# More products of a constant in TensorE's waits, in a four-layer recurrent block of attention and gated layers

## Time and profile before

| | us |
|---|---|
| median of 3 runs | 4672.91 (4669.56 to 4678.95) |
| the profiled execution | 4681.39 |
| its span | 4679.6 |
| mean granted clock of TensorE in the span | 0.924 |
| TensorE busy | 3769.4 (81%) |
| VectorE busy | 2666.6 (57%) |
| ScalarE busy | 1891.5 (40%) |
| GpSimd busy | 782.5 (17%) |

### The profile page before, as it was taken

The page is one execution under the profiler, slowest core; times in us unless marked ns, Lnnn a source line. Parts: engine busy times, 40 slices in busy tenths (PEclk is TensorE's granted clock), DMA queues, the critical chain, the costliest instruction groups (busy, mean ns, idle before and its releaser), DMA issues. The chain is left out here.

```text
span 4679.6 us, 57461 instructions
## 1 busy us (share of the span) xinstructions
PE 3769.4 (81%) x20191; PEld 1899.0 (41%) x20355; DVE 2666.6 (57%) x5719; ACT 1891.5 (40%) x3814; POOL 782.5 (17%) x715
## 2 busy tenths in 40 slices
PE   5878888788887888887887888877888787887776
PEld 2344433435334443344433444343533444334434
DVE  5565556555566545664556555655556654566455
ACT  2443444343433434343344433444343343434324
POOL 0031101220012300222003120032101230012213
PEclk9989998999989999899998999899998999989987
DMA  4000010000000001000100001000000000100030
GB/s 139 28 8 22 5 34 28 15 14 11 28 28 28 1 18 36 20 22 1 39 28 8 22 5 34 28 9 21 11 28 28 28 1 16 36 23 22 1 81 19
DMA packets 79876, 113.86 MB, mean 24 GB/s; under 512 B 11452, under 2 KB 60167, under 8 KB 79047
## 3 DMA queue, kind: packets, MB, share of 16 engines
q1 hardware_dynamic: 73662, 101.08, 7.0%
q10 hardware_dynamic: 5898, 8.77, 0.6%
HBM read 80.68 MB, written 28.34 MB: 23 GB/s over the span
## 5 line engine op out<-in xcount | busy, mean ns | idle before, releaser
L704 DVE TENSOR_REDUCE nmax<-banks 128x1 f32<-128x512 f32 (+3 forms) x1216 | 761.1, 658 | 376.1 <-PE banks L543 208.9
L634 ACT ACTIVATE probs<-banks 128x512 f32<-128x512 f32 (+3 forms) x1536 | 673.7, 491 | 493.1 <-PE banks L561 489.9
L93 PE MATMUL banks<-filler,identb 128*128 128x512 bf16 x2384 | 689.3, 413 | 106.3 <-PEq L73 60.5
L543 PE MATMUL banks<-ks,qs 72*128 72x512 bf16 (+3 forms) x1536 | 472.0, 348 | 100.2 <-DVE nmax L704 70.2
L561 PE MATMUL banks<-qs,ks 74*128 74x512 bf16 (+3 forms) x1536 | 488.8, 352 | 39.9 <-ACT probs L634 21.5
L93 PEld LDWEIGHTS banks<-filler,identb 128*128 128x128 bf16 x2536 | 267.9, 107 | 412.2 <-issue 219.5
L599 PE MATMUL banks<-probs,v 128*32 128x512 f32 (+3 forms) x3072 | 352.9, 533 | 54.9 <-DVE att L691 33.4
L671 POOL TENSOR_SCALAR_AFFINE_SELECT probs<-probs 128x512 f32<-128x512 f32 x256 | 206.8, 809 | 1124.1 <-ACT probs L634 1124.1
L543 PEld LDWEIGHTS banks<-ks,qs 72*128 72x128 bf16 x1536 | 142.0, 101 | 427.9 <-DVE nmax L704 280.0
L333 POOL TENSOR_TENSOR rstd<-var,neghalf 128x4 f32<-128x4 f32 x24 | 24.3, 1011 | 1522.0 <-DVE var L261 1522.0
L561 PEld LDWEIGHTS banks<-qs,ks 74*128 74x128 bf16 x1536 | 144.4, 103 | 291.9 <-ACT probs L634 120.5
(11 more groups left out here) (410 smaller groups left out, 6065.8 us busy)
## 6 DMA issues: line engine op xcount, KB each, us to landing
qs<-parts_scratch SPq DMA_DIRECT2D x288, 96.0 KB
ks<-parts_scratch SPq DMA_DIRECT2D x288, 96.0 KB
parts_scratch<-parts SPq DMA_DIRECT2D x48, 384.0 KB, 2.8
qs<-max_parts SPq DMA_DIRECT2D x192, 4.0 KB
x<-in_x SPq DMA_DIRECT2D x9, 256.0 KB, 2.8
w_up_s<-in_w_up ACTq DMA_DIRECT2D x1, 2048.0 KB
x_scratch<-x SPq DMA_DIRECT2D x8, 256.0 KB, 3.7
factor_scratch<-att SPq DMA_DIRECT2D x8, 256.0 KB
```

Of the source, the lines that this page charges most:

```text
L93: nc.tensor.matmul(K.ps[:, bank, :], K.identb[:, :], K.filler[:, :], start=True, stop=True)
L543: mm = nc.tensor.matmul(K.ps[:, b, i * keys:(i + 1) * keys], K.qs[0:72, 4 * g + j, t * P:(t + 1) * P], K.ks[0:72, 4 * g + j, 0:keys], star ...
L634: nc.scalar.activation(probs[:, 4 * (q % QUADS) + m % 4, q0:T], K.ps[:, bank("second", m), q0:T], ACT.Exp, scale=scale).then_inc(exped, 1)
L704: nc.vector.tensor_reduce(nmax[:, t, h:h + len(heads)], K.ps[:, n % 2, 0:len(heads) * keys].rearrange("p (j k) -> p j k", k=keys), AX.X, A ...
```

## The change

The change adds constant products and nothing else; no transfer and no instruction of another engine is altered. In `down` of the experts a wait for an earlier value of the same semaphore is put in front of them. In the attention the wait for the bank that the next second score overwrites is moved in front of three products into that bank. The diff, cut to its lines:

```diff
@@ gated_layer_norm, TensorE
-            keep_busy(nc, K, 3, 18)
+            keep_busy(nc, K, 3, 26)
             for t in range(NT):
                 pe.wait_ge(xn_ready, t + 1)
...
-            keep_busy(nc, K, 3, 3)
+            keep_busy(nc, K, 3, 5)
@@ prepare, TensorE, layer 2
-                    keep_busy(nc, K, 3, 9)
+                    keep_busy(nc, K, 3, 12)
...
+                    keep_busy(nc, K, 3, 3)
                     pe.wait_ge(xrT_ready, 1)
@@ attention, TensorE (waits_first=10 in layer 1, 0 elsewhere)
+                keep_busy(nc, K, 5, waits_first)
                 beside.run(beside.on_tensor, -1)
...
                         mm.then_inc(oturned, 1)
+                        if causal and second:
+                            bank_read("second", second[0])
+                            keep_busy(nc, K, bank("second", second[0]), 3)
...
                             first_scores(n)
                             if causal and s < LAG:
-                                keep_busy(nc, K, 3, 1)
+                                keep_busy(nc, K, 3, 2 if n == first[0] and s else 1)
...
                     for q in weigh:
                         g, k = divmod(q, NT)
+                        if causal and s > 8 * NG + 1:
+                            keep_busy(nc, K, 0, 10 if q == 4 * NG - 1 else 2)
                         if causal:
                             pe.wait_ge(masked, q + 1)
...
                 if wo is not None:
+                    keep_busy(nc, K, 3, 4)
                     pe.wait_ge(att_ready, NG)
...
                     mm.then_inc(att_turned, 1)
+                    keep_busy(nc, K, 3, 3)
                     pe.wait_ge(attT_ready, 1)
@@ local_qkv, TensorE
     def tensor(pe, banks_free=None):
+        if L:
+            keep_busy(nc, K, 3, 4)
...
+        else:
+            keep_busy(nc, K, 3, 3)
         pe.wait_ge(shifted, 2)
...
             if t:
                 pe.wait_ge(v_copied, 3)
-                keep_busy(nc, K, 2, 8)
+                keep_busy(nc, K, 2, 14 if t == NT - 1 else 8)
+            else:
+                keep_busy(nc, K, 6, 8)
             turn(t)
@@ local_attention, TensorE
+                keep_busy(nc, K, 6, 4)
                 scores(0)
                 scores(1)
+                keep_busy(nc, K, 6, 3)
                 for w in range(UNITS):
                     if w + 2 < UNITS:
                         scores(w + 2)
+                    if w == 0:
+                        keep_busy(nc, K, 6, 5)
                     turn(w)
@@ Glu.tensor
+        keep_busy(nc, K, 3, 5)
         for t in range(NT):
             mm = nc.tensor.transpose(...)
...
+        keep_busy(nc, K, 3, 3)
         pe.wait_ge(self.shifted, 2)
...
+                    if self.alone:
+                        keep_busy(nc, K, 3, 3)
                     pe.wait_ge(self.hnT_ready, 1)
...
+                if self.alone:
+                    keep_busy(nc, K, 1, 5)
                 pe.wait_ge(self.hid_ready, 3)
...
         mm.then_inc(self.down, 1)
+        if self.alone:
+            keep_busy(nc, K, 1, 7)
@@ experts, TensorE
                 def down(e):
+                    if e == E3 - 1:
+                        pe.wait_ge(hid_ready, 2 * e + 1)
+                        keep_busy(nc, K, 0, 5)
                     pe.wait_ge(hid_ready, 2 * e + 2)
...
                 down(E3 - 1)
-                keep_busy(nc, K, 0, 14)
+                keep_busy(nc, K, 0, 22)
```

More of the change, by code:

```diff
@@ L472, in run_alone, with attention @@
     K.clear()
-def attention(nc, K, causal, wo=None, bo=None, combine=True, beside=None, after_store=False):
+def attention(nc, K, causal, wo=None, bo=None, combine=True, beside=None, after_store=False,
+              waits_first=0):
     (scored, reduced, turned, hi_ready, lo_ready, masked, rows, scored2, exped, weighed, oT_ready, oturned, vec,
@@ L1268, in __init__ @@
         self.nc, self.K, self.L = nc, K, L
+        self.alone = alone
         (self.back, self.vec, self.var_ready, self.rstd_ready, self.hn_ready, self.turned, self.hnT_ready, self.up,
@@ L1838, in batch_loop @@
                 prepare(nc, K, 1, beside=ffn)
-                attention(nc, K, True, K.w1_o, beside=ffn)
+                attention(nc, K, True, K.w1_o, beside=ffn, waits_first=10)
         with ExitStack() as two:
```

## The result

| | before | after |
|---|---|---|
| median | 4675.93 us (4 runs, 4669.56 to 4682.99) | 4754.03 us (4 runs, 4750.02 to 4763.5) |
| profiled execution | 4681.39 | 4750.02 |
| granted clock, mean of the span | 0.924 | 0.967 |
| TensorE busy | 3769.4 | 3991.6 |

The changed kernel takes 1.017 times as long (95% interval 1.0147 to 1.0192), some 78 us more. The forecast was 4713 us, some 40 more, with 4755 as the upper end of its range. The direction was right, and the loss is twice the forecast one.

What follows compares the result with a forecast made beforehand. A batch was taken as a chain through TensorE with short waits for others. Costs 17.3 less gains 12.3 gave +5.0 us a batch, 40 in eight: 4672.9 + 40 = 4713 us, own range 4690 to 4735, all cases 4658 to 4755.

Steps and rivals of the forecast that it cites:

- (1): Layer 2's causal attention: no cold stretch in its body, so added products only cost, 6.0 us a batch.
- (f): A batch's start: 6.8 us at low clock slow only 13 products, so a gain of 0.5 us a batch.
- (d): Normalized projections of layer 2 and the experts' start: cold stretches removed, gains of 1.0 and 1.6 us a batch.
- (4): Products that are a block's first work, operands ready after the barrier: 17 x 0.22 = 3.7 us cost a batch.
- (a): Start of layer 1, cold for 10.24 us: first scores must await their rows, so a gain of 1.4 us.
- (2): Layer 1's causal attention: products under busy VectorE are free, the rest cost 4.6 us a batch, 3.6 at the end.
- (b): Layer 1's second cold 10.24 us: 18.88 us against 16.21 for layer 2's same steps, a gain of 2.7 us.
- (c): Layer 1 behind the 2.71 us wait for VectorE: TensorE's chain cold 3.4 or 6.8 us, a gain of 1.9 us.
- Rival A: Faster, chance 0.22: cold stretches are dearer than forecast, net -2.8 us a batch, 4650 us.
- (3): Last turn of each local projection: six more products on the path cost 1.3 us, twice 2.6 a batch.
- Rival C: Clearly slower, chance 0.20: clock still falls at layer 1's two cold stretches, some products outlast waits: 4754 us.
- B: No change, chance 0.13: other engines' waits absorb the attention's products, costs fall by 5 us a batch: 4673 us.

Runs made afterwards that it cites:

- twelve alone: Kernel before with 12 products ahead of the first scores of each local attention: 4732.53 us, ratio 1.012.
- waits-only kernel: Changed kernel without the 102 products a batch shown on the path or beside layer 2's attention, the other 121 kept: 4628.56 us, ratio 0.9905.
- Eleven products: Kernel before with two products, not one, at the first score of each of layer 1's steps 1 to 11: 4655.25 us, ratio 0.9953.
- two mirror runs: Products at the experts' end: changed kernel with 14 instead of 22, 4756.45 us; kernel before with 22 instead of 14, 4681.31 us.
- the 40 alone: Kernel before with only the 40 added products in the body of layer 2's causal attention: 4747.5 us, ratio 1.0149.
- six and eleven products at the right two places: Kernel before with two products before each of layer 1's blocks 10, 11, 12: ratio 0.9939; with eleven in layer 1's steps 1 to 11: 0.9953.

## Why the prediction was half right

**What failed: the size of the sum.** Forecast +5.0 us a batch, measured +8.6. The steps that were mis-sized are (1), 6.0 and measured 7.2; (f), -0.5 and measured +0.6; the experts' part of (d), -1.6 and measured -0.75; and by less (4), 3.7 for 4.2, (a) and (e). Layer 1's attention gave 0.8 us back against them. Two errors stand behind these. The sum let every cold stretch that the products aim at go in all eight trips and let none come in a new place; the changed kernel has one at the start of layer 2's attention in two trips, in the experts' first part in four, at layer 1's start in three, and in its steps 12 to 24 in two. And (f) took idle time behind a barrier for a wait.

**Right: what bounds the kernel and that waits are the measure.** A product on the path costs 0.215 us (twelve alone), one in a wait nothing (twelve more in a wait of 3.12 us), and neither the number of products nor the clock decides alone: the waits-only kernel has 121 of them more than the kernel before, about the changed kernel's clock, and is 1% faster.

**Step (1), mis-sized: 6.0, measured 7.2, which is 6.35 and 0.85 that it did not have.** The ten before the last weighing were right (the last weighing starts 1.85 us later, forecast 1.9), and so were the 1.4 for the first steps with one turn's 0.6: in a trip without a cold stretch, up to the fourth group's first scores, the section grew from 37.1 to 39.1 us. What was a little too small is "the others": from that point to the last turn it is 4.3 us more against 0.6 + 1.9 + 1.5 = 4.0. The remaining 0.85 is a mean over trips: in two of eight the changed kernel has a cold stretch at the start of this attention, and takes 75.7 and 75.3 us. The forecast counted the cold stretches that go and none that come.

**Step (2) with (b) and (c), right but for the size of (c).** The end's costs are 3.9 for 3.6. (c) is 2.6 for 1.9. The steps 12 to 24, where the forecast had (b) less group 0's 0.6, are 2.1 us shorter in the mean, as forecast, but as a mix of 2.9 in six trips and nothing in two. Eleven products brought (b) alone, 3.4 us in seven of eight trips, a little over the 2.7 taken from the same steps of layer 2. Over the first steps the attention lost 0.9 and not 0.4. Rival A, faster by dearer cold stretches, failed on this: a cold stretch of TensorE costs what the same work at full clock saves, less what another engine's wait covers, not half its length.

**Steps (3) and (5), right, (4) nearly.** 2.7 for 2.6 and 0.4 for 0.4. In (4) the local blocks' fours cost 0.8 to 0.86 each, as counted; the lone gated block's five came to 1.6 instead of 1.1, as they ran cold in some trips.

**Step (a), 1.1 for 1.4.** The bound was the right one, a DMA ends the wait. But the rows land 9.6 us after the first issue, 749.61 to 759.23, and not the 9.0 taken from layer 2.

**Step (d), half failed.** The projections gave 1.05 of 1.0. The experts' first part is still cold in four of eight trips, where the forecast let it be warm in all: 0.75 of 1.6.

**Step (f), failed in its mechanism.** It put eight products into 5.53 us <-issue as into a wait. That is time behind a barrier: it starts when the last engine arrives. TensorE was the last already, by 0.3 us, so nothing was free. Forecast -0.5, measured +0.6 in its section; that this counts in the whole the two mirror runs did not show.

**The offset.** The forecast took 8.5 us off for the profiled execution of before standing above its median of three runs (5.5 above that of all four). The changed kernel's profiled execution stood 4 below its own. So of the 41 us between 4713 and 4754, 3.6 x 8 = 29 are the steps above, and 12 are where two single executions lie among their runs.

**Rival C had the number, and its mechanism only in a small part.** It gave 4754 because the clock would still fall in (a) and (b), which were to lose 4.1 us of gains. The clock does still fall there, but in few trips: (a) is cold for about 5 us in three of eight, (b) for 6.8 in two. (a) brought 1.1 for 1.4, and (b)'s steps gave in the mean what was forecast. That its figure is the measured one is luck. The loss is mostly products on the path at full clock, the forecast's own mechanism, with gains that were smaller than forecast. B, that other engines' waits absorb layer 2's products, is excluded by its section, 65.7 to 72.1 us with the 40 alone.

**The signs named ahead.** The batch's clock, 0.98 for 0.97; the last weighing, 1.85 for 1.9; layer 2's section, 6.3 for 6; layer 1's stretch, 15.8 for 16; the local projection's last turn, 1.29 for 1.3: as said. Two were off: the first scores of layer 1 come 7.4 us after the turn of x in the trip shown and 7.0 in the mean, not 6.8, and TensorE's busy time rose by 26 us in the batch shown, not over 30, as products at full clock took the place of cold work.

## What to carry to other kernels

Keep TensorE's clock up with constant products only where the trace shows an idle time that another engine or a DMA ends, one product per 0.216 us of it and no more; in front of each place ask what TensorE does next if the products are not there. Here 102 of 223, all but five of them without such a wait, cost more than all 223 gained, and turned a kernel that is 1% faster into one that is 1.7% slower; six and eleven products at the right two places brought 0.6% and 0.5% alone. Idle time behind a barrier is not a wait: products ahead of it are free only as long as another engine arrives later than TensorE, and here TensorE was the last already.

## What the runs showed that I had not expected

- Cold stretches move. Eleven products that made layer 1's middle warm left its end with the longer cold stretch in five trips and not three, and products in layer 2 alone changed layer 1's mean by 0.5 us. A section without a cold stretch repeats to a hundredth of a microsecond (65.72 and 65.70; 72.06 and 72.06), yet its mean over the trips does not (65.9 and 66.5; 73.1 and 72.3), and the sum of a kernel's sections drifts by one or two us a batch.
- The runs of one kernel lie wider than the first three showed: 4664 to 4689 us for the kernel before on one chip, 4642 to 4667 for one of the changed ones. With 0.2% taken for no change, the chances were drawn somewhat too sharp.
- Half the clock is not half the speed for the chain. The cold time fell by 398 us between the two kernels, and by the runs the gains (layer 1's 4.7, the table's (a), (d) and (e)) are 10.5 us a batch or 84 us in all: 0.21 us for each cold one, where the forecast used up to 0.49. Much of the cold time lay under VectorE or in constant products. The Trainium skill ("TensorE: Matmul & The Clock Gate", "What's actually happening") puts the ramp penalty under 1% of a typical kernel's span; these 84 us are 1.8% of the span here, with 313 us still cold, so the runs don't agree with it for this kernel, which has short cold stretches all over each batch.
